# Head pairs on row halves and a ring of three banks in the second attention of a two-layer transformer kernel

## Chip, cores and metric

The kernel is one launch on one core of a Trainium2 chip. The metric is the device time of that launch in microseconds (us), lower is better. Engines are named as the profile names them: PE is TensorE's matmuls, PEld its weight loads, DVE VectorE, ACT ScalarE, POOL GpSimd, SPq the queue on which SyncE issues its DMAs. "Bank" is one of the eight PSUM banks of 128 partitions x 512 fp32.

## The reference, cut to what matters

Six stages in a row, each with a residual and a LayerNorm: attention, cross attention, a mixture of experts (layer 0), then attention, cross attention and a quantized feed-forward (layer 1). The change is in the fourth:

```python
# B, N, C = 2, 1024, 256; NUM_HEADS = 16, HEAD_DIM = 16, SCALE = 0.25
qkv = (x @ W_qkv + b_qkv).reshape(B, N, 3, NUM_HEADS, HEAD_DIM)
q, k, v = transpose(qkv, (2, 0, 3, 1, 4))
scores = einsum('bhqd,bhkd->bhqk', q, k) * SCALE
attn = softmax(scores, axis=-1)
out = einsum('bhqk,bhkd->bhqd', attn, v)
return out.transpose(0, 2, 1, 3).reshape(B, N, C) @ W_proj + b_proj
# x = layernorm(x + that)
```

## The kernel before, in words

Every stage has one function per engine (`pe_l1a`, `act_l1a`, `dve_l1a`, `pool_l1a`, `sp_l1a` for this one), and the order on each engine is the order of the code; semaphores alone tie the engines together. The stage runs 32 heads (2 batches x 16). Per head it does three things.

**Natural scores**, queries on partitions: only to find each query's largest score. `natural(x, half)` on PE writes 128 queries x 512 keys to bank 0 or 1, DVE reduces it to a column (`L1523`); after 16 of those one small reduce (`L1529`) gives the 8 columns of a head. PE transposes them ("rows", `L1305`), ACT (`L1433`) and DVE (`L1569`) split them into a high and a low part, and SPq sends both as rows into the head's query tile (`L1663`). There they meet a row of ones in the key tile, so that the next product comes with the maximum subtracted.

**Transposed scores**, keys on partitions: two matmuls of 512 queries into banks 2 and 3, or 4 and 5, and one ACT exponential over both banks (`L1440`, 128x1024) into one of three tiles `s_P`.

**Weighting**: `V1` holds 32 columns per head: 16 values, a one in column 16, zeros. Four matmuls of 256 queries, one on each 32-column group of the array, add up into bank 6 over the 8 key tiles. An fp32 matmul stands in the trace as two records, so a unit has 8. Row 16 of each group is the sum of the exponentials. ACT (`L1447`) and DVE (`L1578`) copy bank 6 into `Zs`, 32 rows per head.

A score is summed from four products (high and low part of q with high and low part of k): the query and key tiles `Qs` and `Ks` of a head carry four copies on 4 x 32 partitions, gathered by eight DMAs from the projected `TQK` (`L1645`). All matmuls of scores so use 128 rows.

A step x of the loop is a *unit*: one of 8 key or query tiles of one head, 256 in all. PE does in this order: natural half 0, transposed scores of unit x-13, natural half 1, weighting of unit x-15, then a side piece of the list `side[x]`, if there is one. Side pieces all go through bank 7, one after the other: projection of the next four heads (28 pieces in the loop, six 512-column matmuls each, evacuated by ACT `L1407` and DVE `L1503`), the values of batch 1, the rows, and for every group of four heads "sums" (the sums turned, PE then DVE reciprocal `L1546`), "spread" (ACT `L1422`), "scale" (PE turns back, DVE `L1550` multiplies), and once per batch the output projection in four groups ("project", DVE `L1554`) and the LayerNorm steps ("norm"). What is left when the loop ends runs as `rest` behind it, with the transposes `turned` of the normalized X for the next stage (four for batch 0, four for batch 1).

PE's helper `mm` is line 85, so nearly all matmuls stand under L85 and are told apart by their tiles: `PS<-s_K,s_Q` is natural, `PS<-s_Q,s_K` transposed, `PS<-s_P,s_V` the weighting.

Of the kernel before, what the change touches and what calls it, by code (L numbers as in the profile page):

```python
# [25 lines left out]
              "m_gh m_h7 m_gT c_l0 rows c_xb m_b7 m_r1 m_w1 m_r2 s_wrl s_w s_z1 s_wpl s_g0 s_g1 s_g2 s_g3 s_nr s_i s_n "  # L26
              "s_red s_za s_zv s_b7 s_rx sums s_p7 s_ip s_exp s_st s_pv s_hi s_mhd f_l0 f_l1 f_iv f_qv s_xb f_qp x_lk x_kv "
              "x_lv x_vd x_pl x_ql x_q x_fp x_ft x_ev x_z x_lo x_zT x_o x_n0 x_n1 x_t x_K0 x_K1 x_min x_s x_qh x_sub x_ex "
              "x_kT x_lh x_res f_max x_rcp x_mx x_lq x_lm f_dv f_sp f_xr f_xq f_xt f_h f_gu f_hq f_y f_yp f_cl f_e4 f_sil "
              "f_up f_hr f_hpr f_sm f_par f_s1 f_res f_hp dve").split()  # L30
# [43 lines left out]
def program(nc, A, out):  # L74
    ctx = ExitStack()
    with ctx:
# [53 lines left out]
        s_wp = sb(ctx, "s_wp", [128, 4, D])  # L130
        s_bm = sb(ctx, "s_bm", [128, 128])
# [37 lines left out]
        R_S = 4  # L169
        Qs = [sb(c, f"s_Q{i}", [128, S], FR) for i in range(R_S)]  # L170
        Ks = [sb(c, f"s_K{i}", [128, S], FR) for i in range(R_S)]
        Zs = [sb(c, f"s_Z{i}", [128, 4, S]) for i in range(2)]
        s_P = [sb(c, f"s_P{i}", [128, S]) for i in range(3)]
        nm2 = sb(c, "s_nm2", [128, 2, 8, 2])
        s_nm = sb(c, "s_nm", [128, 2, 8])
        s_mh, s_ml = sb(c, "s_mh", [8, 2, 128], FR), sb(c, "s_ml", [8, 2, 128], FR)
        s_rc = sb(c, "s_rc", [128, 2, 32])
        s_rx = [sb(c, f"s_rx{i}", [128, 512]) for i in range(2)]
# [963 lines left out]
        def pool_rest(e):  # L1142
# [25 lines left out]
            for n in sorted(plan):  # L1168
                for what in plan[n]:
                    if what[0] == "weights":  # L1170
                        split(what[1] + 3)
                    elif what[0] == "prepare":
                        e.wait_ge(s["m_y"], last_of[-1])
                        for i, (hi, lo) in enumerate(((s_vh, s_vl), (s_wh, s_wl))):
                            e.wait_ge(s["s_wrl"], 16 * (i + 1))
                            e.tensor_copy(hi[:, :], s_wr[:, :]).then_inc(s["s_w"], 1)
                            e.wait_ge(s["s_w"], 2 * i + 1)
                            e.tensor_tensor(lo[:, :], s_wr[:, :], hi[:, :].bitcast(F32), ALU.subtract).then_inc(s["s_w"], 1)
                        e.memset(V1[:, :, :, 16:32], 0.0).then_inc(s["s_z1"], 1)
                        e.wait_ge(s["s_z1"], 1)  # L1180
                        e.memset(V1[:, :, :, 16:17], 1.0).then_inc(s["s_z1"], 1)

        def sp_rest(e):
# [19 lines left out]
            for n in sorted(plan):  # L1203
                for what in plan[n]:
                    if what[0] == "weights":
                        load(what[1] + 3)
                    elif what[0] == "prepare":
                        e.wait_ge(s["m_y"], last_of[-1])
                        e.dma_start(s_wp[:, :, :], A["s_wp"].rearrange("(g p) n -> p g n", p=128)).then_inc(s["s_wpl"], 16)
                        e.dma_start(s_bm[:, :], A["s_bm"]).then_inc(s["s_wpl"], 16)  # L1210
# [8 lines left out]
        NH, LAG_M, LAG_S, LAG_P = 32, 9, 13, 15  # L1219
        N_X = 8 * NH + LAG_P  # L1220
# [4 lines left out]

        side, todo = [[] for _ in range(N_X)], []
        for x in range(N_X):
            if 0 <= x - LAG_M < 8 * NH and (x - LAG_M) % 8 == 0:
                side[x].append(("rows", (x - LAG_M) // 8))
            y = x - LAG_P  # L1230
            if 0 <= y < 8 * NH:
                if y // 8 == 15:
                    side[x].append(("values", y % 8))
                if y % 32 == 31:
                    pb, pg = y // 128, (y // 32) % 4
                    todo += [("sums", pb, pg), ("spread", pb, pg), ("scale", pb, pg, 0), ("scale", pb, pg, 1)]
                    if pg == 3:
                        for q in range(2):
                            todo += [("project", 8 * pb + j) for j in range(4 * q, 4 * q + 4)]
                            todo.append(("norm", 8 * pb + 4 * q))  # L1240
            if todo and x // 8 % 4 > 1 and x % 8 in (3, 5, 7):
                side[x].append(todo.pop(0))
            n, i = divmod(x, 8)
            if i in (2, 6) and n % 4 < 2 and n // 4 + 1 < 8:
                side[x].append(("proj", n // 4 + 1, 2 * (n % 4) + (i == 6)))
        rest = todo
        i7, i7_free, bank7 = {}, {}, {}
        for what in [w for row in side for w in row]:
            if what[0] not in ("spread", "norm"):
                i7[what], i7_free[what], bank7[what] = len(i7) + 1, len(i7), 7  # L1250
        before = {7: len(i7), 6: None}
        for i, what in enumerate(rest):
            if what[0] not in ("spread", "norm"):
                bank7[what], i7_free[what] = 7 - i % 2, before[7 - i % 2]
                i7[what] = before[7 - i % 2] = len(i7) + 1
        n_sums = {what: i for i, what in enumerate(w for w in i7 if w[0] == "sums")}

        def his(g):

            return 4 * g  # L1260

        def pe_l1a(e):
# [17 lines left out]
            def natural(x, half):  # L1280
                z, (n, i) = 2 * x + half, divmod(x, 8)
                if i == 0 and half == 0:
                    e.wait_ge(s[f"s_g{n % 4}"], 128 * (n // 4 + 1))
                if z >= 2:
                    e.wait_ge(s["s_nr"], z - 1)
                else:
                    e.wait_ge(s["s_i"], 12)
                mm(e, PS[:, half, :], Qs[n % R_S][:, i * 128:(i + 1) * 128],
                   Ks[n % R_S][:, half * 512:half * 512 + 512], True, True).then_inc(s["s_n"], 1)

            def piece(what):
# [12 lines left out]
                if what[0] == "rows":
                    t = e.transpose(PS[0:8, 7, 0:128], s_nm[:, what[1] % 2, :], ident[:, :])  # L1305
                elif what[0] == "values":
                    e.wait_ge(s[who_old], n_old)
                    t = values(1, what[1], 7)
                elif what[0] == "proj":
# [3 lines left out]
                    t = proj(g, u, 7)  # L1313
                elif what[0] == "sums":
                    _, b, g = what
                    e.wait_ge(s["s_za"], 2 * (16 * b + 4 * g + 4))
                    e.wait_ge(s["s_zv"], 2 * (16 * b + 4 * g + 4))
                    e.wait_ge(s["s_wpl"], 32)
                    for j in range(8):
                        t = mm(e, PS[:, bk, 4 * j:4 * j + 4], Zs[b][:, g, j * 128:(j + 1) * 128], s_bm[:, 16:128:32], True, True)  # L1320
                elif what[0] == "scale":
                    _, b, g, half = what
                    e.wait_ge(s["s_rx"], 2 * n_sums["sums", b, g] + half + 1)
                    for j in range(4):
                        t = mm(e, PS[:, bk, j * 128:(j + 1) * 128], s_rx[half][:, j * 128:(j + 1) * 128], ident[:, :], True, True)
                else:
                    b, j = divmod(what[1], 8)
                    e.wait_ge(s["s_b7"], i7["scale", b, 3, 1])
                    e.wait_ge(s["s_wpl"], 32)
                    for g in range(4):  # L1330
                        t = mm(e, PS[:, bk, 0:256], Zs[b][:, g, j * 128:(j + 1) * 128], s_wp[:, g, :], g == 0, g == 3)
# [5 lines left out]
            for u in range(4):  # L1337
                if u >= 2:
                    e.wait_ge(s["s_i"], u - 1)
                proj(0, u, u % 2).then_inc(s["s_ip"], 1)  # L1340
            for kt in range(8):
                e.wait_ge(s["s_i"], kt + 3)
                values(0, kt, kt % 2).then_inc(s["s_ip"], 1)
            for x in range(N_X):
                if x < 8 * NH:
                    natural(x, 0)
                extra = list(side[x])
                if extra and extra[0][0] == "rows":
                    piece(extra.pop(0))
                w = x - LAG_S  # L1350
                if 0 <= w < 8 * NH:
                    h, kt = divmod(w, 8)
                    bk = (2, 4)[w % 2]
                    if kt == 0:
                        e.wait_ge(s[f"row{h % 2}"], 256 + 32 * (h // 2 + 1))
                    if w >= 2:
                        e.wait_ge(s["s_exp"], w - 1)
                    for half in range(2):
                        t = mm(e, PS[:, bk + half, :], Ks[h % R_S][:, kt * 128:(kt + 1) * 128],
                               Qs[h % R_S][:, half * 512:half * 512 + 512], True, True)  # L1360
                    t.then_inc(s["s_st"], 1)
                if x < 8 * NH:
# [897 lines left out]
```

## Time and profile before

| | us |
|---|---|
| median of 3 runs | 2763.31 |
| lowest, highest | 2759.94, 2772.22 |
| the profiled execution, its time | 2767.74 |
| its span in the profile | 2765.9 |
| first natural matmul of the stage | at 1894.0 |
| last weighting matmul | ends at 2441.0 |
| last normalized tile of the stage | at 2479.1 |

The span is what the profile shows from the first to the last instruction; the execution's time has 1.8 us around it. Over the whole span PE is busy 91%, DVE 62%, ACT 46%, POOL 31%. A record's duration of a matmul has a latency in it: a 512-column matmul stands as 0.39 to 0.40 us but the next can start 0.22 to 0.23 us after it, so starts are to be read, not durations. The mean granted clock of TensorE over the span is 0.955 of full speed.

### The profile page before, as it was taken

To read this page: it belongs to the slowest core of one execution; us is meant where nothing else is said; L and a number is where in the kernel's file an instruction comes from. 1 tells how busy PE (TensorE), PEld (TensorE's weight loads), DVE (VectorE), ACT (ScalarE), POOL (GpSimd) and SP (SyncE) were. 2 spreads that over 40 slices of the span, in tenths; PEclk is the share of its full clock that TensorE was granted. 3 is DMA by queue.
4 is the path that set the end of the run, shared out by engine and by line. 5 is a ranking of instruction groups with operands and counts; after the bars stand their busy time and mean duration, and the time that the engine had idled before them with its cause. 6 is when DMAs were issued, how large, how long until landed. Compare 5 with 4: busy or idle time off the path is not lost.

```text
span 2765.9 us, 35667 instructions
## 1 busy us (share of the span) xinstructions
PE 2511.4 (91%) x13840; PEld 1727.1 (62%) x13840; DVE 1717.4 (62%) x3089; ACT 1282.2 (46%) x2015; POOL 867.3 (31%) x445
## 2 busy tenths in 40 slices
PE   8999998999999789899999999997999999976663
PEld 7554545744554579788888988994555555544421
DVE  5566655376665446875444344356877777847967
ACT  4555554345555144344444444442666555632342
POOL 4777774366777240102222023010200000004323
PEclk9999999999999899899999999998999999987885
DMA  2000001000000210000000010003333232210000
GB/s 74 12 22 14 12 12 43 12 12 23 12 19 1 69 61 1 31 1 31 31 31 20 12 43 9 1 1 83 74 66 70 62 66 62 47 32 9 1 0 31
DMA packets 49641, 84.23 MB, mean 30 GB/s; under 512 B 9912, under 2 KB 30016, under 8 KB 49472
## 3 DMA queue, kind: packets, MB, share of 16 engines
q1 hardware_dynamic: 49328, 81.88, 11.6%
q8 instruction: 110, 1.80, 0.3%
q14 instruction: 59, 0.48, 0.1%
q10 hardware_dynamic: 144, 0.07, 0.0%
HBM read 37.49 MB, written 2.10 MB: 14 GB/s over the span
## 4 chain that ended last, share of the span: by engine, by line
PE 75%; DVE 16%; ACT 3%; issue 3%; POOL 2%; DMA 1%; SPq 0%; ACTq 0%; DVEq 0%; POOLq 0%
PE PS L85 74%; DVE m_gl L1097 2%; DVE PS L576 2%; DVE a_QS L554 1%; ACT a_P L519 1%; DVE a_nm L568 1%; DVE s_nm L1523 1%; DVE X L271 1%; DVE x_E L1922 1%; DVE x_rd L1906 1%; DVE st_s L232 1%; DVE x_sm L1927 1%; POOL f_H L2128 1%; POOL a_sum L676 1%; ACT a_QS L473 1%
## 5 line engine op out<-in xcount | busy, mean ns | idle before, releaser
L1097 DVE TENSOR_TENSOR m_gl<-m_g,m_gh 128x512 fp32r<-128x512 f32 x288 | 258.1, 902 | 386.4 <-ACT m_g L936 386.4
L676 POOL TENSOR_TENSOR a_sum<-a_sum,a_P 128x1024 f32<-128x1024 f32 x192 | 456.6, 2378 | 128.4 <-ACT a_P L519 118.0
L519 ACT ACTIVATE a_P<-PS 128x512 f32<-128x512 f32 x512 | 290.3, 596 | 354.3 <-PE PS L85 349.5
L933 ACT ACTIVATE m_gh<-PS,cols 128x512 fp32r<-128x512 f32 x288 | 198.5, 689 | 469.6 <-PE PS L85 469.6
L1523 DVE TENSOR_REDUCE s_nm<-PS 128x1 f32<-128x512 f32 x512 | 344.8, 688 | 70.0 <-PE PS L85 67.4
L568 DVE TENSOR_REDUCE a_nm<-PS 128x1 f32<-128x1024 f32 x256 | 300.4, 1216 | 128.2 <-PE PS L85 128.2
L85 PE MATMUL PS<-m_w2h,m_gh 128*128 128x256 f32 x1152 | 324.5, 282 | 18.9 <-DVE m_gl L1097 18.7
L1440 ACT ACTIVATE s_P<-PS 128x1024 f32<-128x1024 f32 x256 | 262.1, 1024 | 165.4 <-PE PS L85 164.8
L85 PE MATMUL PS<-m_w2l,m_gh 128*128 128x256 f32 x1152 | 323.1, 280 | 0.0
L85 PE MATMUL PS<-m_w2h,m_gl 128*128 128x256 f32 x1152 | 323.0, 280 | 0.0
L85 PE MATMUL PS<-a_P,a_V 128*64 128x512 f32 x1024 | 250.9, 612 | 0.0
L85 PEld LDWEIGHTS PS<-m_w2h,m_gh 128*128 128x128 f32 x1152 | 217.7, 189 | 35.3 <-DVE m_gl L1097 23.7
L85 PE MATMUL PS<-s_K,s_Q 128*128 128x512 f32 x512 | 229.4, 450 | 8.8 <-DVE s_nm L1523 6.1
L85 PE MATMUL PS<-xh,m_w1h 128*128 128x512 f32 x576 | 231.5, 402 | 0.0
L85 PE MATMUL PS<-xh,m_w1l 128*128 128x512 f32 x576 | 227.2, 394 | 0.0
L85 PE MATMUL PS<-a_QS,a_KH 128*128 128x512 f32 x512 | 219.9, 430 | 7.8 <-ACT a_P L519 7.7
L85 PE MATMUL PS<-xl,m_w1h 128*128 128x512 f32 x576 | 226.1, 393 | 0.0
L85 PEld LDWEIGHTS PS<-m_w2h,m_gl 128*128 128x128 f32 x1152 | 218.5, 190 | 10.7
L85 PEld LDWEIGHTS PS<-m_w2l,m_gh 128*128 128x128 f32 x1152 | 218.1, 189 | 0.0
L1152 POOL CAST m_w1h<-m_raw 128x2048 fp32r<-128x2048 f32 x9 | 20.0, 2223 | 609.3 <-PE PS L85 599.9
L85 PE MATMUL PS<-a_QM,a_KL 128*128 128x512 f32 x512 | 201.8, 394 | 0.0
L936 ACT ACTIVATE m_g<-PS,cols 128x512 f32<-128x512 f32 x288 | 196.7, 683 | 0.0
(304 smaller groups left out, 4346.8 us busy)
## 6 DMA issues: line engine op xcount, KB each, us to landing
m_raw<-in_m_w SPq DMA_DIRECT2D x16, 1024.0 KB, 5.2
s_Q<-s_T SPq DMA_DIRECT2D x128, 128.0 KB, 2.4
s_K<-s_T SPq DMA_DIRECT2D x128, 128.0 KB, 2.4
a_KH<-a_KH SPq DMA_DIRECT2D x64, 128.0 KB, 2.3
a_wr<-in_w_qk SPq DMA_DIRECT2D x16, 256.0 KB, 2.9
X<-in_x SPq DMA_DIRECT2D x4, 512.0 KB, 6.6
a_P<-in_w_v SPq DMA_DIRECT2D x8, 256.0 KB, 5.8
a_P<-in_w_o SPq DMA_DIRECT2D x2, 1024.0 KB, 5.5
```

The source lines that it names most:

```text
L85: return e.matmul(o, l, r, start=start, stop=stop, skip_group_check=shared)
L232: e.bn_stats(st_s[:, j, :], X[:, j, :]).then_inc(own.sem, 1)
L271: e.tensor_scalar(X[:, j, :], X[:, j, :], st_a[:, j, 0:1], st_r[:, 0, j:j + 1], ALU.subtract, ALU.mult).then_inc(s["normed"], 1)
L519: e.activation(a_P[:, g % N_P, half * 512:half * 512 + 512], PS[:, 2 + half, :], ACT.Exp).then_inc(s["a_exp"], 1)
L568: e.tensor_reduce(a_nm[:, n % 2, 8 * a + i:8 * a + i + 1], PS[:, bk:bk + 2, :], AX.XY, ALU.max, negate=True).then_inc(s["a_max"], 1)
L576: e.reciprocal(r, r).then_inc(own.sem, 1)
L676: e.tensor_tensor(o[:, :], a_P[:, (g - 1) % N_P, :] if k == 1 else o[:, :], a_P[:, g % N_P, :], ALU.add).then_inc(s["a_add"], 1)
L933: e.activation(m_gh[r][:, :], PS[:, 4 + n % 3, :], func, bias=cols[:, bcol:bcol + 1]).then_inc(s["m_gh"], 1)
L936: e.activation(m_g0[r][:, :], PS[:, 4 + n % 3, :], func, bias=cols[:, bcol:bcol + 1]).then_inc(s["m_g0"], 1)
L1097: e.tensor_tensor(m_gl[r][:, :], m_g0[r][:, :], m_gh[r][:, :].bitcast(F32), ALU.subtract).then_inc(s["m_gl"], 1)
L1440: e.activation(s_P[w % 3][:, :].rearrange("p (a n) -> p a n", a=2), PS[:, bk:bk + 2, :], ACT.Exp, scale=0.25).then_inc(s["s_exp"], 1)
L1523: e.tensor_reduce(nm2[:, n % 2, i, half:half + 1], PS[:, half, :], AX.X, ALU.max, negate=True).then_inc(s["s_nr"], 1)
```

## The change

- **Head pairs.** A unit is now half a tile of a *pair* of heads, 256 units for 16 pairs. `Qs` and `Ks` hold one head on partitions 0 to 63 and the other on 64 to 127 (`R[0]`, `R[1]`), with 32 + 16 + 16 rows of high and low parts; the product of the two low parts is left out. Each score matmul has 64 rows. A natural unit is two matmuls, one on each row half, into a pair of banks, and one DVE reduce over 128x1024 in place of two over 128x512.
- **Ring.** The transposed scores of a unit are two matmuls (one for each head), each into the next of banks 4, 5 and 7, each with its own wait for the exponential three before it; ACT does two exponentials over 128x512, into four tiles `s_P`.
- **Weighting** in two units at a time, every second step: 2 x 4 matmuls, column group c for head c % 2 and query quarter c // 2. `V1` has ones in columns 16 to 31, so that the sum comes out sixteenfold on 16 partitions beside the 16 values. One ACT copy (128x256) per half pair into `s_zt`; then eight DMAs per pair bring values to `Zs` and sums to `Zd`, both packed 8 heads to 128 partitions.
- **Division.** DVE inverts `Zd` in pieces of 128 columns (24 in the loop, 4 of 256 behind it), POOL multiplies (`Zs` by `Zd`), for the last group DVE. "sums", "spread" and "scale" are gone, and `s_bm`; a project piece does two tiles with two groups each in place of one with four.
- **Banks.** Natural units and all side pieces except the rows take turns on the bank pairs 0-1 and 2-3; the rows go to bank 6, columns 256 to 383.
- **Lags** 16 and 18 in place of 13 and 15, so 274 steps. Only the high part of the rows is sent; `L1569` goes. The first four `turned` are side pieces now.
- **DMAs on SPq** per pair: 12 to gather (before 2 x 8), 4 for rows (before 4), 8 for `Zs` and `Zd` (before none).

The diff, cut to PE's loop, ACT's exponentials, DVE's reduce and SPq's DMAs behind each pair, in this order:

```diff
-        NH, LAG_M, LAG_S, LAG_P = 32, 9, 13, 15
-        N_X = 8 * NH + LAG_P
+        N_PR, LAG_S, LAG_P = 16, 16, 18
+        N_U = 16 * N_PR
+        N_X = N_U + LAG_P
+        RING = (4, 5, 7)
...
+            if x % 32 in (3, 7, 11, 15) and x // 32 + 1 < 8:
+                side[x].append(("proj", x // 32 + 1, (x % 32) // 4))
+            if x % 64 in range(22, 38, 2) and 86 <= x < 278:
+                side[x].append(("inverse", (x - 86) // 64, (x % 64 - 22) * 64, 128))
...
+                    who = {"natural": "s_nr", "turned": "t_xl"}.get(what[0], "s_b7")
+                    pair[what], pair_free[what], n_b7[what] = 2 * (len(used) % 2), used[-2], count[who]
...
+            for x in range(N_X):
+                w = x - LAG_S
+                if 0 <= w < N_U:
+                    p, half, kt = w // 16, (w // 8) % 2, w % 8
+                    if kt == 0:
+                        e.wait_ge(s[f"row{(w // 8) % 2}"], 256 + 32 * (w // 16 + 1))
+                    for a in range(2):
+                        if 2 * w + a >= 3:
+                            e.wait_ge(s["s_exp"], 2 * w + a - 2)
+                        mm(e, PS[:, RING[(2 * w + a) % 3], :], Ks[p % R_S][R[a], kt * 128:(kt + 1) * 128],
+                           Qs[p % R_S][R[a], half * 512:half * 512 + 512], True, True).then_inc(s["s_st"], 1)
+                if x < N_U:
+                    bk, (who, n) = pair["natural", x], pair_free["natural", x]
+                    e.wait_ge(s[who], n)
+                    for a in range(2):
+                        t = mm(e, PS[:, bk + a, :], Qs[p % R_S][R[a], i * 128:(i + 1) * 128],
+                               Ks[p % R_S][R[a], half * 512:half * 512 + 512], True, True)
+                    t.then_inc(s["s_n"], 1)
+                y = x - LAG_P
+                if y % 2 and 0 < y < N_U:
+                    for y in (y - 1, y):
+                        e.wait_ge(s["s_exp"], 2 * y + 2)
+                        for c in range(4):
+                            part = 512 * (c % 2) + 256 * (c // 2)
+                            t = mm(e, PS[32 * c:32 * c + 32, 6, 0:256], V1[:, kt, (h + c % 2) % 16, :],
+                                   s_P[y % 4][:, part:part + 256], kt == 0, kt == 7)
+                        t.then_inc(s["s_pv"], 1)
+                for what in side[x]:
+                    piece(what)
...
+                    for a in range(2):
+                        e.wait_ge(s["s_st"], 2 * w + a + 1)
+                        e.activation(s_P[w % 4][:, a * 512:a * 512 + 512], PS[:, RING[(2 * w + a) % 3], :],
+                                     ACT.Exp, scale=0.25).then_inc(s["s_exp"], 1)
...
+                    e.tensor_reduce(nm2[:, p % 2, :, i, half], PS[:, bk:bk + 2, :], AX.X, ALU.max,
+                                    negate=True).then_inc(s["s_nr"], 1)
...
+                    for c in range(4):
+                        o, sub = 32 * (p % 4) + 16 * (c % 2), c // 2
+                        for dst, r in ((Zs[g // 2], 32 * c), (Zd, 32 * c + 16)):
+                            dst = dst[o:o + 16, g % 2, :].rearrange("p (h n) -> p h n", h=2)
+                            e.dma_start(dst[:, :, sub * 256:sub * 256 + 256], s_zt[r:r + 16, q:q + 2, :]).then_inc(s[f"s_zd{p % 2}"], 16)
```

## Rows read from the trace of the kernel before

**Rows 1.** Busy time by stretch: start:end, length, five engines, granted clock, DMA share, GB/s.
```profile
1894.00:1918.00 24.00, 18.19 (x45) 9.83 (x45) 18.39 (x31) 3.62 (x5) 0.00 (x0) 0.86 0.71 168
1918.00:2426.00 508.00, 501.96 (x3423) 274.57 (x3423) 402.32 (x737) 303.96 (x375) 24.75 (x24) 1.00 0.28 62
...
2441.00:2479.20 38.20, 26.37 (x140) 22.32 (x136) 20.09 (x70) 5.26 (x10) 0.00 (x0) 0.89 0.00 1
2479.20:2560.00 80.80, 53.64 (x218) 39.05 (x219) 58.58 (x86) 22.10 (x38) 33.66 (x20) 0.73 0.13 35
```

**Rows 2.** Timeline of PE over one plain unit: start us, duration us, instructions.
```profile
2072.14 0.64 PE L85 MATMUL PS<-s_P,s_V 128*32 128x256 f32 x8
2072.71 0.50 PE L85 MATMUL PS<-s_K,s_Q 128*128 128x512 f32 x1
2073.05 0.63 PE L85 MATMUL PS<-s_Q,s_K 128*128 128x512 f32 x2
2073.51 0.40 PE L85 MATMUL PS<-s_K,s_Q 128*128 128x512 f32 x1
2073.83 0.42 PE L85 MATMUL PS<-s_P,s_V 128*32 128x256 f32 x4
```

**Rows 3.** Groups of the loop, 1894 to 2441.2: count, busy us, mean ns, idle before.
```profile
L1523 DVE TENSOR_REDUCE s_nm<-PS 128x1 f32<-128x512 f32 x512 | 344.8, 688 | 70.0 <-PE PS L85 67.4
L1440 ACT ACTIVATE s_P<-PS 128x1024 f32<-128x1024 f32 x256 | 262.1, 1024 | 165.4 <-PE PS L85 164.8
...
L85 PEld LDWEIGHTS PS<-s_K,s_Q 128*128 128x128 f32 x512 | 96.7, 189 | 111.5 <-DVE s_nm L1523 78.3 <-issue 20.2 <-DMA s_K<-s_T 1.7
...
L1503 DVE SCALAR_TENSOR_TENSOR s_T<-PS,cols,s_T 128x512 fp32r<-128x512 f32 x28 | 20.8, 742 | 0.0
L1407 ACT ACTIVATE s_T<-PS,cols 128x512 fp32r<-128x512 f32 x28 | 19.3, 691 | 51.1 <-PE PS L85 51.1
L85 PE MATMUL PS<-s_wp,s_Z 128*128 128x256 f32 x64 | 16.0, 392 | 0.0
L85 PE MATMUL PS<-ident,s_rx 128*128 128x128 f32 x96 | 13.9, 288 | 0.0
L85 PE MATMUL PS<-s_bm,s_Z 128*128 128x4 f32 x112 | 13.6, 254 | 0.0
...
L1529 DVE TENSOR_REDUCE s_nm<-s_nm 128x8 f32<-128x16 f32 x32 | 5.4, 170 | 1.1
```

**Rows 4.** Timeline of the loop's end, where no natural scores are left.
```profile
2437.32 0.73 PE L85 MATMUL PS<-s_Q,s_K 128*128 128x512 f32 x2
2437.98 0.64 PE L85 MATMUL PS<-s_P,s_V 128*32 128x256 f32 x8
2438.09 1.03 ACT L1440 ACTIVATE s_P<-PS 128x1024 f32<-128x1024 f32 x1 [0.21 <-PE PS L85]
2438.55 0.73 PE L85 MATMUL PS<-s_Q,s_K 128*128 128x512 f32 x2
2439.22 1.82 PE L85 MATMUL PS<-s_P,s_V 128*32 128x256 f32 x24
```

**Rows 5.** Groups of the whole span, by shape, that other stages show.
```profile
L568 DVE TENSOR_REDUCE a_nm<-PS 128x1 f32<-128x1024 f32 x256 | 300.4, 1216 | 128.2 <-PE PS L85 128.2
L576 DVE RECIPROCAL PS<-PS 128x256 f32<-128x256 f32 x64 | 108.1, 1733 | 48.7 <-PE PS L85 48.3
L519 ACT ACTIVATE a_P<-PS 128x512 f32<-128x512 f32 x512 | 290.3, 596 | 354.3 <-PE PS L85 349.5
```

**Rows 6.** DMAs that read the projected tiles: ns min/median/max of an issue, landing time.
```profile
L1645 SPq DMA_DIRECT2D s_Q<-s_T x128: 521/590/2152, 1887.1 to 2387.7; - x128
...
DMA to landing us min/median/max: 2.3/2.4/4.1
```

**Rows 7.** Timeline behind the loop, its two ends: the last copies and the last normalization.
```profile
2441.11 0.89 DVE L1578 COPY s_Z<-PS 32x256 f32<-32x256 f32 x2 [8.49 <-PE PS L85]
...
2468.72 0.75 DVE L1554 TENSOR_TENSOR X<-PS,X 128x256 f32<-128x256 f32 x2
...
2477.73 1.38 DVE L271 TENSOR_SCALAR X<-X,st_a,st_r 128x256 f32<-128x256 f32 x4
```

More of the change, by code:

```diff
@@ L1227, in program @@
         for x in range(N_X):
-            if 0 <= x - LAG_M < 8 * NH and (x - LAG_M) % 8 == 0:
-                side[x].append(("rows", (x - LAG_M) // 8))
+            if x >= 9 and (x - 9) % 8 == 0 and (x - 9) // 8 < 2 * N_PR:
+                side[x].append(("rows", (x - 9) // 8))
             y = x - LAG_P
[L1231 to L1240, printed above, removed]
@@ L1241, in program @@
-            if todo and x // 8 % 4 > 1 and x % 8 in (3, 5, 7):
-                side[x].append(todo.pop(0))
[L1243 to L1260, printed above, removed]
+            if y % 2 == 1 and 120 <= y < 128:
+                side[x].append(("values", y - 121))
@@ new lines, in program @@
+            if x in (229, 237, 245, 253):
+                side[x].append(("turned", (x - 229) // 8))
+        rest = []
+        for i in range(4):
+            rest += [("inverse", 3, 256 * i, 256), ("divide", 256 * i), ("project", 8 + 2 * i)]
+        rest = [rest[i] for i in (0, 1, 3, 4, 2, 6, 7, 5)] + [("norm", 8)] + [rest[i] for i in (9, 10, 8, 11)] + [("norm", 12)]
+        i7, pair, pair_free, n_b7, used = {}, {}, {}, {}, [("s_i", 12), ("s_i", 12)]
+        count = {"s_b7": 0, "s_nr": 0, "t_xl": 16}
@@ new lines, in dve_l1a @@
+            for x in range(N_X):
+                if x == 40:
+                    slow.append(round_steps(e, own, range(6)))
+                if x < N_U:
+                    p, i, half = x // 16, (x // 2) % 8, x % 2
+                    e.wait_ge(s["s_n"], x + 1)
+                    if x % 16 == 0 and p >= 2:
+                        e.wait_ge(s["s_red"], 2 * p - 2)
+                    bk = pair["natural", x]
+                    e.tensor_reduce(nm2[:, p % 2, :, i, half], PS[:, bk:bk + 2, :], AX.X, ALU.max,
+                                    negate=True).then_inc(s["s_nr"], 1)
+                    if x % 8 == 7:
+                        q = x // 8
+                        e.wait_ge(s["s_nr"], x + 1)
+                        if q >= 2:
+                            e.wait_ge(s["s_p7"], i7["rows", q - 2])
+                        e.tensor_reduce(s_nm[:, q % 2, :].rearrange("p (a i) -> p a i", a=2),
+                                        nm2[:, p % 2, :, 4 * (q % 2):4 * (q % 2) + 4, :], AX.X, ALU.min).then_inc(s["s_red"], 1)
+                if late:
+                    what = late.pop()
+                    if what[0] == "turned":
+                        turned(what[1], pair[what])
+                    else:
+                        low(what[1], what[2], pair[what]).then_inc(s["s_b7"], 1)
+                for what in side[x]:
+                    piece(what)
+                pump(slow, 2)
@@ L1589, in dve_l1a @@
             pump(slow, 99)
-            for i in range(4):
-                turned(i, i % 2)
             for what in rest:
```

442 lines of the change are left out of this document (183 added, 259 removed).

## The prediction

> **What bounds the kernel now.** First the busy time by stretch [rows 1]. From 1918 to 2426 us PE is busy 502 of 508 us at full granted clock, DVE 402, ACT 304. This stage is 547 us from its first natural matmul to its last weighting, and PE is its wall. Then the groups [rows 3]: ACT's exponentials waited 165 us for PE, DVE's reduces 67 us for PE, PE next to nothing for others. Then one plain unit, by starts and not by durations [rows 2]: weighting at 2072.14, the two transposed and two natural matmuls in between, weighting again at 2073.83, so 1.69 us a unit. A 512-column matmul behind a like one takes 0.22 to 0.23 (2073.05 to 2073.51 is two), the change from 128x128 to 128x32 tiles 0.33 (2073.51 to 2073.83), so 0.11 of it is the switch. Where natural scores are gone a unit takes 1.23 [rows 4].
>
> These make up the loop: lead-in 24.0 [rows 1], 243 units at 1.69 = 410.7, last 15 at 1.23 = 18.5; 547.1 less these leaves 93.9 for all side pieces. That agrees with what PE does there: 28 projections of 6 matmuls at 0.23 = 38.6, sums, scale and project 13.6 + 13.9 + 16.0 = 43.5 [rows 3], the rest rows and values.
>
> **The change part by part.**
>
> *What PE has to do in two units.* Weighting: 24 records in a row take 1.82, and the last one's latency is some 0.16 of it, so 8 take 0.55 and 16 take 1.10 [rows 4]. Score pairs on row halves: no row shows two matmuls on different rows at once. Bounds: 0.22 a pair (fully side by side, as the four column groups of the weighting are: eight 256-column fp32 records in 0.57 [rows 2, 4]) and 0.43 (one after the other). I take 0.22, because the nearest row, the column groups, does overlap. The Trainium skill, "TensorEngine Tiling (Array Packing)", Key Properties, says that different tiles load weights and run matmuls in parallel, and that changing the mode drains the array. By it a pair is 0.22; the drain agrees with the 0.11 of rows 2, overlap of rows no trace here shows.
>
> *What ACT and DVE have to do.* A unit has two exponentials of 512 at 596 ns = 1.19 us [rows 5] in place of one of 1024 ns [rows 3]; DVE one reduce of 1216 ns [rows 5] in place of 2 x 688 = 1.38 [rows 3]. So ACT needs 2.38, DVE 2.43 for two units, PE 4 x 0.22 + 1.10 + 2 switches = 2.2 to 3.1. None is the wall by far; PE's fixed order then is.
>
> *The chain through the ring.* Put the end of exponential (w-1, head 0) at 0, w odd in the order of weighting. It frees the bank for (w, head 1). PE: start 0.1 (semaphore, an estimate: from PE's end at 2438.05 to ACT's start it was 0.04 [rows 4], and a weight load comes first), 0.32 the natural pair, 0.54 switch, 0.66 weighting of two units 1.10, switch 0.10, next unit's transposed scores at 1.86. Their exponential can start 0.43 later (a record's 0.39 plus the semaphore), at 2.29, and ends at 2.89. ACT had only 1.79 us of scores in the three banks, so it idles 0.5. The exponential ending at 2.89 frees the bank for (w+2, head 1), which is where we began. **Period 2.89 for two units, 1.445 a unit.** DVE needs 2.43 in it and fits. Without the natural pair it is 2.67, 1.33 a unit.
>
> *Side pieces.* 93.9 less sums and scale 27.5, less half of the project pieces 8.0 [rows 3]. Plus one more switch (0.11) for each of 28 projections and 32 rows, 6.6; plus four transposes moved in, 2.4; plus 24 inversions on DVE of half of 1733 ns = 20.8 [rows 5], of which DVE's slack hides half (0.46 us per two units): 10.4; plus LayerNorm and rounding steps on a DVE with less slack, 8 (estimate); plus ACT's row and bank-6 copies beyond its idle 0.5, 5. Sum 91. A projection now takes a turn on the natural banks: low part 742 ns [rows 3] on DVE and a natural unit one turn later; inside the 1.4 us that PE is away DVE has one reduce pending, so I charge nothing more. It costs up to 1 us each, 28 us, if the buffers run dry; that is in the range.
>
> *Loop.* Lead-in: 16 units without exponentials at DVE's pace, 16 x 1.27 (1.216 and a gap of 0.05) = 20.3, plus 6 for its projections (before: 24.0 less 13 x 1.38). Middle 240 x 1.445 = 346.8. Sides 91. End 18 x 1.33 = 23.9. Together 488, against 547.1: **-59**.
>
> *Start.* The first natural unit now waits for 12 gathers, not 8; SPq issues one every 0.63 (0.59 and a gap) [rows 6]: **+2.5**.
>
> *Behind the loop.* Before, 38 us from the last weighting to the last normalized tile [rows 7], DVE busy 20 [rows 1]. Now: ACT copy 0.6, eight DMAs 5.1, landing 2.4 [rows 6], then DVE with four inversions of 1733 (6.9), four products (1.5), and what it did, less the four `turned` and the scaling, some 15: 31.6. **-6**, between -10 and +3 (PE cold in the DMA wait).
>
> *DMAs and POOL.* SPq issues 24 per pair = 15.1 us, of 23.1 for 16 units. The rows of the second half queue behind 12 gathers (7.6), take 1.3 to issue and 2.4 to land: 11.3 after step 15 of the pair, wanted nine units later, at 13.0. Hidden, with 1.7 to spare; at 1.25 us a unit it would not be. POOL's products are off the chain: it was busy 25 of 508 us [rows 1], and a project piece that needs one comes many units later. Dropping `L1569` and the 32-partition copies relieves DVE, which isn't the wall: nothing. `L1529` stays, 32 x 170 ns.
>
> **Sum:** -59 + 2.5 - 6 = -62.5 against the profiled execution, 2767.7 (span 2765.9 and 1.8 around it), so 2705; that execution stood 4.4 above the median 2763.3, so **2701 us**.
>
> **The rivals.**
>
> *B, pairs don't overlap.* A pair takes 0.43, whether the array or the weight loads serialize it: each load stands as 189 ns [rows 3] and a pair has two. The chain grows by 0.22 per two units to 3.11, 1.555 a unit: +26, 2727. For it: no row shows the overlap, and the loads stay 128 columns wide. Against: the column groups.
> The Trainium skill, "TensorE: Matmul & The Clock Gate", LDWEIGHTS, says that a load's time goes by columns and not by rows, 107 ns for 128; halving the rows then saves no load time. By that figure two loads fit under one 0.22 matmul and the period stays 1.445. The trace has loads of 189 as recorded, but with their latency, so it doesn't decide.
>
> *C, the chain is slacker than I draw it* and DVE's own work is the wall: 256 x 1.216 = 311, low parts 21, small reduces 5, inversions 21, others about 25: 383, plus the last 18 units 24 = 407. -140 and the ends: 2620. For it: the ring holds 1.79 us of exponentials, and two natural units can be pending. Against: in-order PE must finish 1.1 us of weighting between two banks.
>
> *D, slower: the clock falls.* For the first time in this loop PE would wait often. The mean granted clock was 1.00 where PE is busy 99%, 0.86 at 76%, 0.89 at 69%, 0.73 at 66% [rows 1]; the two levels are 2.4 and 1.2 GHz. PE's part of the chain, 1.86 of 2.89, doubles at 1.2: +0.93 a unit. With half of the loop at 1.2: +112, sides +36, so 2849. The change is lost once the period passes 1.705 (62.5 / 240 more), that is with 28% of the loop at 1.2. Against: in the lead-in's 76% busy most is recorded latency, two starts of 0.22 in 1.38 us; here starts fill 2.2 of 2.89.
>
> *E, SPq is late.* The eight new DMAs cut 16 partitions into 1 KB pieces, which no row shows. At the 0.59 median they fit. At the longest issue seen, 2.15 [rows 6], a pair needs 17.2 + 10.1 = 27.3 us against 23.1: +67 over 16 pairs, 2768, no change. It decides from about 1.6 us an issue.
>
> **How the numbers follow.** Forecast 0.50, B 0.20, C 0.13, D 0.06, E 0.08; 0.03 for anything else on the faster side. A measurement of this kernel can tell about 0.5% (14 us). Faster: 0.50 + 0.20 + 0.13 + 0.03 = 0.86; same 0.08 (E); slower 0.06 (D). The range 2640 to 2745 takes in the bounds of the forecast (sides -10 to +28, pair 0.22 to 0.43, tail -4 to +9), all of B and the near half of C; it leaves out D, E and the rest of C, 0.2.
>
> **What would show it.** Right: plain pairs of units repeat every 2.9 us; ACT's exponentials at 596 idle about 0.5 us every second unit, released by PE; the two matmuls of a natural pair start within 0.05 us; PE near 80% busy at clock 1.00; last weighting some 490 us after the first natural matmul. B: starts within a pair 0.22 apart, period 3.1 or more. C: reduces back to back at 1.22. D: granted clock under 0.9. E: PE's waits released by the DMA of `s_mh` or by the gathers, 2 us and more per half pair. A period above 3.4 us for two units with none of these would break the account of the chain itself.

## The result and the profile after

12 runs each, side by side: 2766.57 us before, 2776.44 after (2771.68 to 2785.24), ratio 1.0039 with a 95% interval of 1.0024 to 1.0054. The change is **slower by 0.4%**; the forecast was 2701 with a range of 2640 to 2745. The profiled execution of the changed kernel has a span of 2779.9, 14.0 more than before.

Busy time by stretch, changed kernel (columns as in rows 1): lead-in up to the first transposed matmuls, loop, its end, and what lies behind it up to the next stage.

```profile
1900.90:1936.00 35.10, 23.94 (x62) 12.16 (x62) 21.59 (x22) 3.98 (x6) 1.49 (x2) 0.60 0.23 55
1936.00:2436.00 500.00, 428.25 (x3117) 205.56 (x3121) 347.94 (x401) 279.21 (x568) 30.75 (x29) 0.89 0.21 41
2436.00:2459.40 23.40, 19.29 (x195) 8.12 (x193) 1.40 (x2) 17.39 (x35) 0.00 (x0) 1.00 0.05 12
2459.40:2490.50 31.10, 13.25 (x44) 9.82 (x40) 18.18 (x47) 0.98 (x3) 0.00 (x0) 0.71 0.04 9
```

Against [rows 1] PE, DVE and ACT have less to do (PE 428 us of 500 where it had 502 of 508), only POOL has more (31 us where it had 25). Yet the loop did not get shorter, and the granted clock, 1.00 before, is 0.89 on average, in the lead-in 0.60 for 0.86. Where the 14.0 us are:

| stretch | before | after | difference | forecast |
|---|---|---|---|---|
| last matmul of the stage before starts | 1867.8 | 1872.7 | +5.0 | 0 |
| from there to the first natural matmul | 26.2 | 28.2 | +2.0 | +2.5 |
| first natural to end of last weighting | 547.1 | 558.5 | +11.4 | -59 |
| to the last normalized tile | 38.1 | 34.8 | -3.3 | -6 |
| rest of the kernel | 286.8 | 285.7 | -1.1 | 0 |

The first line is scatter of the unchanged stages between executions: in the profile of one of the kernels below that same matmul starts at 1860.4. Start and tail came as forecast, within 3 us. The loop is 70 us off.

The exponentials and reduces on the page of the changed kernel:

```profile
L1525 DVE TENSOR_REDUCE s_nm<-PS 128x2 f32<-128x1024 f32 x256 | 310.2, 1219 | 142.8 <-PE PS L85 142.2
L1408 ACT ACTIVATE s_P<-PS 128x512 f32<-128x512 f32 x512 | 264.4, 602 | 102.9 <-PE PS L85 102.7
```

1219 and 602 ns, against 1216 and 596 taken from [rows 5]: the prices were right. DVE now waits 142 us for PE (67 before, rows 3): the engine that makes the others wait is still PE, though it is itself idle. So who makes PE wait? First two plain units, timeline of the changed kernel (one line of ACT, the rest PE):

```profile
2108.57 1.07 PE L85 MATMUL PS<-s_P,s_V 128*32 128x256 f32 x16
2109.57 0.50 PE L85 MATMUL PS<-s_Q,s_K 64*128 64x512 f32 x2
2109.91 0.40 PE L85 MATMUL PS<-s_K,s_Q 64*128 64x512 f32 x2
2110.14 0.39 PE L85 MATMUL PS<-s_Q,s_K 64*128 64x512 f32 x1
2110.16 2.07 ACT L1408 ACTIVATE s_P<-PS 128x512 f32<-128x512 f32 x4 [1.99 <-PE PS L85]
...
2110.81 0.49 PE L85 MATMUL PS<-s_Q,s_K 64*128 64x512 f32 x1 [0.28 <-ACT s_P L1408]
2110.82 0.71 PE L85 MATMUL PS<-s_K,s_Q 64*128 64x512 f32 x2
2111.46 1.07 PE L85 MATMUL PS<-s_P,s_V 128*32 128x256 f32 x16
```

From 2108.57 to 2111.46 is 2.89 us, the forecast's 2.89. Two matmuls on the two row halves stand as one line of 0.50 or 0.40, and the next kind starts 0.23 to 0.34 later: they overlap in full. The wait of 0.28 is for the exponential that frees the next bank of the ring. This is the chain, and it is the whole of a plain pair of units. Now a pair with a projection and the one behind it:

```profile
2029.81 1.07 PE L85 MATMUL PS<-s_P,s_V 128*32 128x256 f32 x16
2030.81 0.50 PE L85 MATMUL PS<-xh,s_wh 128*128 128x512 f32 x1
...
2032.39 0.51 PE L85 MATMUL PS<-s_Q,s_K 64*128 64x512 f32 x2
2032.50 0.69 ACT L1390 ACTIVATE s_T<-PS,cols 128x512 fp32r<-128x512 f32 x1 [1.94 <-PE PS L85]
...
2033.17 1.23 DVE L1525 TENSOR_REDUCE s_nm<-PS 128x2 f32<-128x1024 f32 x1 [2.03 <-PE PS L85]
2033.73 0.49 PE L85 MATMUL PS<-s_Q,s_K 64*128 64x512 f32 x1 [0.37 <-ACT s_P L1408]
2034.31 0.74 DVE L1467 SCALAR_TENSOR_TENSOR s_T<-PS,cols,s_T 128x512 fp32r<-128x512 f32 x1
2035.11 0.50 PE L85 MATMUL PS<-s_K,s_Q 64*128 64x512 f32 x2 [0.89 <-DVE s_T L1467]
2035.54 1.93 PE L85 MATMUL PS<-s_P,s_V 128*32 128x256 f32 x16
...
2037.40 0.79 PE L85 MATMUL PS<-s_Q,s_K 64*128 64x512 f32 x2
...
2039.62 1.07 PE L85 MATMUL PS<-s_P,s_V 128*32 128x256 f32 x16
```

This takes 5.73 us (2.83 above plain), and the pair behind it 4.08. Read it from the wait of 0.89 backwards: the natural matmuls need the bank pair in which the projection lies; DVE reads it last (`L1467`, 2034.31 to 2035.05); but DVE's order has the next natural reduce first (2033.17), which PE could only feed after the projection. Everything in the pair waits in a ring. Then the weighting at 2035.54 lasts 1.93 and not 1.07. Busy time of the same stretches:

```profile
2029.81:2035.54 5.73, 4.47 (x32) 2.31 (x31) 3.21 (x4) 3.39 (x7) 0.00 (x0) 1.00 0.61 129
2035.54:2039.62 4.08, 4.08 (x27) 1.77 (x25) 2.18 (x2) 1.33 (x3) 0.00 (x0) 0.58 0.23 53
2039.62:2045.35 5.73, 4.47 (x31) 2.31 (x30) 3.45 (x5) 3.37 (x7) 0.00 (x0) 1.00 0.03 6
2045.35:2049.56 4.21, 4.21 (x27) 1.87 (x25) 2.42 (x2) 2.10 (x6) 0.00 (x0) 0.59 0.00 1
```

The granted clock, the number behind the five engines, is 1.00 with the projection and 0.58 to 0.59 behind it: most of that pair ran at the lower of the two levels, 1.2 GHz. Of the 24 pairs behind a projection in the loop 17 have a clock of 0.57 to 0.72; the other 7 have 1.00. Five of these stand behind a pair of the same 5.73 to 5.74 us, the plain pair at 2108.57 above among them. So the clock does not fall behind every such stop, and nothing here says behind which. By the starts of the weightings, the 24 pairs of units in the loop that carry a projection take 6.33 us on average, the 24 behind them 3.94; by the forecast's terms a projection alone makes it 4.4 (2.89, 1.38 for six matmuls, 0.11 for a switch) and 2.9. In the kernel below that has neither this wait nor the next one the same pairs take 4.77 and 3.15, other side pieces included, so 24 x 2.3 = 56 us are waits and slow clock.

A last stall, once in each of three groups of heads; waits in the loop of the changed kernel:

```profile
DVE s_Zd L1499 <- DMA s_Zd<-s_zt: 13.4, 3, 4.9
```

and the first of the three in the timeline:

```profile
2081.89 0.95 DVE L1499 RECIPROCAL s_Zd<-s_Zd 128x128 f32<-128x128 f32 x1 [4.82 <-DMA s_Zd<-s_zt]
...
2083.98 0.80 PE L85 MATMUL PS<-s_K,s_Q 64*128 64x512 f32 x2 [4.28 <-DVE s_nm L1525]
```

The first inversion of a group comes in DVE's order before its sums have landed, and PE stands 4.3 us behind DVE.

So there are three theories: **1**, the shared natural banks and DVE's order behind them; **2**, the clock that falls behind most of these stops; **3**, the late DMA. The rival to all is that the side pieces and the inversions simply cost more work.

### The profile page after: what moved, and what is told of

Same layout as the page of the kernel before. It is cut to its first block, busy times and chain, and to the rows that moved or that the text cites. A ratio compares the mean times of both kernels' runs of the same rounds, so it can differ in the third digit from the quotient of the medians.

```text
span 2779.9 us, 34891 instructions
## 1 busy us (share of the span) xinstructions
PE 2436.5 (88%) x13518; PEld 1651.5 (59%) x13520; DVE 1672.6 (60%) x2737; ACT 1259.5 (45%) x2223; POOL 873.8 (31%) x450
## 4 chain that ended last, share of the span: by engine, by line
PE 70%; DVE 18%; ACT 4%; issue 3%; SPq 2%; POOL 1%; DMA 1%; ACTq 0%; DVEq 0%; POOLq 0%
PE PS L85 68%; DVE m_gl L1096 2%; DVE s_nm L1525 2%; DVE PS L575 2%; ACT s_P L1408 2%; DVE a_QS L553 1%; ACT a_P L518 1%; DVE a_nm L567 1%; SPq L1605 1%; DVE X L270 1%; DVE x_E L1894 1%; DVE x_rd L1878 1%; DVE s_T L1467 1%; SPq L1637 1%; DVE x_sm L1899 1%
## 5 line engine op out<-in xcount | busy, mean ns | idle before, releaser
L1525 DVE TENSOR_REDUCE s_nm<-PS 128x2 f32<-128x1024 f32 x256 | 310.2, 1219 | 142.8 <-PE PS L85 142.2
L567 DVE TENSOR_REDUCE a_nm<-PS 128x1 f32<-128x1024 f32 x256 | 300.4, 1216 | 127.1 <-PE PS L85 127.1
L1408 ACT ACTIVATE s_P<-PS 128x512 f32<-128x512 f32 x512 | 264.4, 602 | 102.9 <-PE PS L85 102.7
L85 PE MATMUL PS<-s_Q,s_K 64*128 64x512 f32 x512 | 188.6, 512 | 35.6 <-ACT s_P L1408 35.3
L85 PE MATMUL PS<-s_K,s_Q 64*128 64x512 f32 x512 | 148.8, 481 | 55.3 <-DVE s_T L1467 27.2
```

The source lines that it names most:

```text
L85: return e.matmul(o, l, r, start=start, stop=stop, skip_group_check=shared)
L567: e.tensor_reduce(a_nm[:, n % 2, 8 * a + i:8 * a + i + 1], PS[:, bk:bk + 2, :], AX.XY, ALU.max, negate=True).then_inc(s["a_max"], 1)
L1408: e.activation(s_P[w % 4][:, a * 512:a * 512 + 512], PS[:, RING[(2 * w + a) % 3], :], ACT.Exp, scale=0.25).then_inc(s["s_exp"], 1)
L1525: e.tensor_reduce(nm2[:, p % 2, :, i, half], PS[:, bk:bk + 2, :], AX.X, ALU.max, negate=True).then_inc(s["s_nr"], 1)
```

## The experiments

Each edit is against the changed kernel if nothing else is said. "Plain" and "projection" are the pairs of units from weighting to weighting, read as above.

### The low part first

```diff
                 elif what[0] == "proj":
-                    late.append(what)
+                    low(what[1], what[2], pair[what]).then_inc(s["s_b7"], 1)
```

> Edit: DVE takes the low part of a projection (the read that frees the natural bank pair) before the next natural reduce, not behind it. Theory 1 (shared natural banks): a step pair with a projection takes 5.73 us in the changed kernel's trace where a plain one takes 2.90; 1.5 of the 2.83 is PE's own work and the rest the wait for that low part. It ends about 1.1 us earlier here: step pair about 4.6, PE's wait for the low part from 0.89 to under 0.2, stage 28 x 1.1 = 31 us shorter, 2745. If the clock also stays up behind it (theory 2), the following step pair falls from 4.1 to about 3.0 as well, 2715. Rival (the shared banks don't matter, PE's extra work does): 5.73 stays, 2776.

2725.44, ratio 0.9861 (0.9827 to 0.9895): 50 us less by moving 28 instructions of DVE one place forward.

```profile
2021.35 1.07 PE L85 MATMUL PS<-s_P,s_V 128*32 128x256 f32 x16
...
2024.76 0.75 DVE L1467 SCALAR_TENSOR_TENSOR s_T<-PS,cols,s_T 128x512 fp32r<-128x512 f32 x1 [1.88 <-ACT s_T L1390]
2025.27 0.50 PE L85 MATMUL PS<-s_Q,s_K 64*128 64x512 f32 x1 [0.37 <-ACT s_P L1408]
...
2025.57 0.49 PE L85 MATMUL PS<-s_K,s_Q 64*128 64x512 f32 x2
2025.99 1.07 PE L85 MATMUL PS<-s_P,s_V 128*32 128x256 f32 x16
...
2029.10 1.07 PE L85 MATMUL PS<-s_P,s_V 128*32 128x256 f32 x16
```

The projection's pair takes 4.64 (expected 4.6), PE no longer waits for the low part, and the pair behind it 3.11, weighting back to 1.07. Theory 1 stands. The clock fell behind none of the 24 projections here, so the 50 us hold what theory 2 has to price as well. The time lies between the two expected numbers: three pairs with late sums are left, and they grew from 7.7, 6.5 and 8.6 us to 9.2, 7.6 and 9.7.

### Filling the wait

```diff
-                        mm(e, PS[:, RING[(2 * w + a) % 3], :], Ks[p % R_S][R[a], kt * 128:(kt + 1) * 128],
-                           Qs[p % R_S][R[a], half * 512:half * 512 + 512], True, True).then_inc(s["s_st"], 1)
+                        for _ in range(4 if a and any(z[0] == "proj" for z in side[x - 2]) else 1):
+                            t = mm(e, PS[:, RING[(2 * w + a) % 3], :], Ks[p % R_S][R[a], kt * 128:(kt + 1) * 128],
+                                   Qs[p % R_S][R[a], half * 512:half * 512 + 512], True, True)
+                        t.then_inc(s["s_st"], 1)
```

> Edit: in the step in which PE waits for the low part of a projection, it runs the transposed matmul of the second head four times into the same bank, so three of them (0.66 us) fill the wait of 0.89 without changing a result. Theory 2 (the granted clock falls behind each projection because PE stands still, 1.00 then 0.58 to 0.60 in the trace, and costs 1.2 us a time): the step pair behind a projection goes from 4.1 to about 2.9, the fourth projection of a group from 7.6 to 5.7, in all some 25 to 35 us less, about 2745, with more matmuls. Rival (the slow pair behind a projection has another cause, such as the banks): no change, or up to 28 x 0.3 = 8 us more.

2747.12, ratio 0.9942 (0.9921 to 0.9963): 29 us *less* by doing *more* matmuls (27 by the two ratios).

```profile
2024.90 1.19 PE L85 MATMUL PS<-s_Q,s_K 64*128 64x512 f32 x4 [0.38 <-ACT s_P L1410]
2026.29 0.50 PE L85 MATMUL PS<-s_K,s_Q 64*128 64x512 f32 x2 [0.19 <-DVE s_T L1469]
2026.72 1.07 PE L85 MATMUL PS<-s_P,s_V 128*32 128x256 f32 x16
...
2029.61 1.07 PE L85 MATMUL PS<-s_P,s_V 128*32 128x256 f32 x16
```

The projection's pair stays at 5.75, since the wait for the low part still ends when it did; the pair behind it takes 2.89 in place of 4.08, and the 7.6 of a group's fourth projection is 5.7. In the loop the clock fell behind 17 of 24 projections before and behind none now, and the banks are as they were, so the slow pairs behind projections are the clock's alone. Theory 2 stands, and its price there is these 27 to 29 us; they are a part of the 50 of the first edit, not added to them.

### Inversions six steps later

```diff
-            if x % 64 in range(22, 38, 2) and 86 <= x < 278:
-                side[x].append(("inverse", (x - 86) // 64, (x % 64 - 22) * 64, 128))
+            if x % 64 in range(28, 44, 2) and 92 <= x < 278:
+                side[x].append(("inverse", (x - 92) // 64, (x % 64 - 28) * 64, 128))
```

> Edit: the 8 inversions of a group start 6 steps later. Theory: in the changed kernel DVE waits 4.8 us in its own order for the DMA of the sums at the first inversion of each of three groups, and PE behind it 4.3 (step pair 7.7 for 2.9), clock 0.52 for 9 us after that. Here that wait is gone: 3 x 4.5 = 13 us, and 3 to 8 more of the clock, 2757 to 2763. Rival (the inversions themselves, 0.94 us of DVE each, are what costs): the stall moves along, under 4 us gained.

2757.32, ratio 0.9969 (0.9952 to 0.9987), 0.7% or 19 us under the changed kernel. The wait on the DMA is gone from the list of waits of the loop, and in two of the three groups plain pairs with an inversion in them take 2.90 us. There the inversions cost nothing; their place did. In the third group, where DVE has LayerNorm steps as well, pairs with an inversion still take 2.9 to 6.5. Theory 3 stands.

### Both natural matmuls on one row half

The maxima of each pair's second head are left out; the first head's are used for it.

```diff
-                        t = mm(e, PS[:, bk + a, :], Qs[p % R_S][R[a], i * 128:(i + 1) * 128],
-                               Ks[p % R_S][R[a], half * 512:half * 512 + 512], True, True)
+                        t = mm(e, PS[:, bk + a, :], Qs[p % R_S][R[0], i * 128:(i + 1) * 128],
+                               Ks[p % R_S][R[0], half * 512:half * 512 + 512], True, True)
```

> Edit: both matmuls of a natural pair read the first row half, so the maxima of the second head are left out and the first head's used in their place; all else as the changed kernel. Theory (row halves overlap; a pair costs PE one 512-column matmul): starts within the pair go from together to 0.22 apart, a plain step pair from 2.90 to about 3.11, the stage 120 x 0.21 = 25 us longer, 2800. Rival (PE has slack enough in a step pair to take it): 2.90 stays, 2776.

2819.93, ratio 1.0201 (1.0165 to 1.0237): 44 more than the changed kernel, but not as expected. Timeline of a plain pair and busy time of its loop:

```profile
2161.97 0.51 PE L85 MATMUL PS<-s_Q,s_K 64*128 64x512 f32 x2
2162.31 0.62 PE L85 MATMUL PS<-s_K,s_Q 64*128 64x512 f32 x2
2162.77 0.94 PE L85 MATMUL PS<-s_Q,s_K 64*128 64x512 f32 x2
```

```profile
1935.00:2480.00 545.00, 491.55 (x3107) 247.93 (x3104) 342.23 (x399) 278.91 (x562) 30.41 (x28) 0.82 0.19 37
```

The two now follow each other (0.62 for 0.40, and the next kind starts 0.46 later where it was 0.23), but a plain pair still takes 2.90 to 2.91. The step of the expectation that fell is that the chain has no room for it. In the second unit the natural pair never was together: its second matmul shares rows with the transposed one of the second head and went behind it already (0.71 at 2110.82 above). In the first unit the added 0.23 came out of PE's wait for the ring: the wait of 0.28 is gone, and the two transposed matmuls of the second unit stand as one line without a gap (2162.77). So this kernel shows the overlap by its absence, but prices neither the expected 25 us nor rival B, in which no pair overlaps. What grew are the pairs with projections (6.2 to 8.5 for 5.7 to 7.7, where no values are computed in them) and the share of the slow clock, 0.82 for 0.89.

### A ring of two, and a bank of their own for the projections

```diff
-        RING = (4, 5, 7)
+        RING = (4, 5)
...
+                elif what[0] == "proj":
+                    count["s_b7"] += 1
+                    pair[what], pair_free[what], n_b7[what] = 7, own7, count["s_b7"]
+                    own7, i7[what] = ("s_b7", count["s_b7"]), len(i7) + 1
...
-                        if 2 * w + a >= 3:
-                            e.wait_ge(s["s_exp"], 2 * w + a - 2)
+                        if 2 * w + a >= 2:
+                            e.wait_ge(s["s_exp"], 2 * w + a - 1)
```

> Edit: the ring of the transposed scores has two banks (4, 5), and bank 7 belongs to the projections, as before the change; the rest is the changed kernel. Theory (the shared natural banks cost the projections their 2.8 us; the ring sets the plain step pair by the chain of the prediction): with two banks the chain is 0.1, 0.22 + 0.22 + 0.12, 1.10 of weighting, 0.10, 0.43 to the next exponential, two exponentials of 0.60, 3.49 us for a plain step pair in place of 2.90, and a step pair with a projection only its own 1.6 longer, near 5.1, with the pair behind it plain. Plain pairs +0.59 x 120 = +71, projections -28 x 1.2 and the clock behind them -28 x 1.0: 2785 in all. Rival (the ring's size doesn't matter): plain stays 2.90, 2715.

2780.19, ratio 1.0055 (1.0037 to 1.0073). Two plain units:

```profile
2003.94 1.07 PE L85 MATMUL PS<-s_P,s_V 128*32 128x256 f32 x16
...
2006.18 0.98 PE L85 MATMUL PS<-s_Q,s_K 64*128 64x512 f32 x2 [0.51 <-ACT s_P L1412]
...
2007.33 1.07 PE L85 MATMUL PS<-s_P,s_V 128*32 128x256 f32 x16
```

Plain 3.39 (expected 3.49), with a projection 5.07 (5.1), behind it 3.40 to 3.60. The third bank is worth 0.49 us on every plain pair, 59 us in 120; a bank of their own for the projections, with the clock that stays up behind them (0.96 in the loop), gives back all but 4 of these. The change traded the one for the other. The same bank shortens the lead-in, 33.3 us in the changed kernel, to about the forecast's 26:

```profile
1888.00:1915.20 27.20, 19.69 (x59) 10.04 (x59) 20.79 (x21) 2.33 (x4) 0.00 (x0) 0.69 0.31 70
```

### One unit of weighting in every step

```diff
-                if y % 2 and 0 < y < N_U:
-                    for y in (y - 1, y):
+                if 0 <= y < N_U:
+                    for y in (y,):
```

> Edit: weighting of one unit in every step, not of two in every second; all else the changed kernel. Theory (the plain step pair is the chain through the ring, in which 1.1 us of weighting stands between two banks): with 0.55 in its place ACT never runs dry, a plain pair becomes PE's own work, 2 x (0.10 + 0.22 + 0.22 + 0.12 + 0.55), 2.45 us instead of 2.90: 120 x 0.45 = 54 us less, 2720, the projections' waits staying. Rival (each switch of tile shape costs more than 0.11, or DVE's 1.22 a unit with its gaps is the wall): 2.7 to 2.9 a pair, 2750 to 2776.

2711.90, ratio 0.9807 (0.9786 to 0.9828), 64 less than the changed kernel (54 expected). PE's work from one start of weighting to the next:

```profile
2002.35 0.64 PE L85 MATMUL PS<-s_P,s_V 128*32 128x256 f32 x8
...
2002.92 0.50 PE L85 MATMUL PS<-s_Q,s_K 64*128 64x512 f32 x2
...
2003.25 0.40 PE L85 MATMUL PS<-s_K,s_Q 64*128 64x512 f32 x2
...
2003.58 0.64 PE L85 MATMUL PS<-s_P,s_V 128*32 128x256 f32 x8
```

1.23 a unit, 2.46 a pair, against 2.45 expected, although the tile shape now changes twice as often, and PE no longer waits in it. DVE's two reduces of 1.22 would allow hardly less. The weighting of two units at once is what let the ring run dry.

### Low part first and late inversions

> Edit: the low part of a projection first on DVE, and the inversions 6 steps later, together. If the two losses are separate stalls they add: 2725 less 13 to 20, so 2708 (in the kernel with the first edit alone three step pairs of 7.6 to 9.7 us were left). Rival (with the first edit the DMA wait is hidden by nothing less and moves to another place): 2725.

2696.61, ratio 0.9756 (0.9739 to 0.9773): 28.8 below the first edit alone, more than the 13 to 20 expected: in the kernel with the first edit alone the three pairs with late sums took 9.2, 7.6 and 9.7 us and the one behind each 4.9, which is 24 above plain. Its natural and its weighting matmuls:

```profile
L85 PE MATMUL PS<-s_K,s_Q x512: 383/394/793, 1894.8 to 2351.5; 64*128 64x512 f32 x171
```

```profile
L85 PE MATMUL PS<-s_P,s_V x2048: 379/379/634, 1931.7 to 2375.0; 128*32 128x256 f32 x187
```

The loop is 480.6 us (1894.8 to 2375.0 and a record's 0.4), where the forecast has 488, and the granted clock in it 0.61 in the lead-in and 0.99 behind. Its pairs with a projection take 4.65, where no values are computed in them; the forecast's terms give 4.4.

### All three

> Edit: all three, one unit of weighting in every step, low part first, inversions late. If chain, bank wait and DMA wait are separate, 2708 less 54 = 2655. Rival (DVE becomes the wall: 256 x 1.22 and 70 us of pieces, 382 us of a loop that is then 440): each piece on DVE shows in full, 2680.

**2662.45, ratio 0.9633 (0.9614 to 0.9651)**, the best but one of the kernels made here, 3.7% under the kernel before. It is 7 us above the 2655 of the expectation. Two entries of its waits, 1930 to 2330:

```profile
DVE s_nm L1525 <- PE PS L85: 16.5, 30, 1.8
...
PEld PS L85 <- DMA s_Q<-s_mh: 9.2, 5, 3.1
```

DVE's reduces wait 17 us where they waited 142: now PE and DVE are close to even (357 and 325 us busy in 375). And PE waits for the DMA of the row of maxima, five times: the forecast has it hidden with 1.7 us to spare at 1.445 a unit and not at 1.25, and at 1.23 it shows.

### The lead-in filled

Against the kernel with all three:

```diff
-                    for a in range(2):
+                    for a in (0, 1) * (4 if x < 16 else 1):
                         t = mm(e, PS[:, bk + a, :], Qs[p % R_S][R[a], i * 128:(i + 1) * 128],
```

> Edit: the kernel with single weighting, low part first and late inversions; in the 16 units of the lead-in, where PE has only natural pairs, each pair is run four times into the same banks, so results stay. Theory (the lead-in takes 31 us because PE stands still behind DVE and the granted clock falls to 0.61, which makes its four projections 1.4 us longer each): clock near 1.00 there, lead-in from 30.9 to about 25 us, 2657 against 2662. Rival (DVE's 16 reduces, the low parts and the waits between them make the 31 us): the repeated matmuls delay each reduce by 0.66 and the lead-in grows to 33 or more, 2665.

2658.53, ratio 0.9625 (0.9606 to 0.9644), which overlaps the interval of the kernel without it. Its lead-in:

```profile
1893.60:1922.50 28.90, 26.82 (x153) 16.70 (x153) 21.61 (x21) 2.33 (x4) 0.00 (x0) 0.92 0.28 65
```

The clock rose from 0.61 to 0.92, but the lead-in fell only from 30.9 to 28.9, not to 25. Both theories hold in part: the first projection takes 1.60 us for 2.86, but the repeated matmuls make the reduces later. Not tried: an order of the lead-in that has fewer waits.

## Why the prediction was wrong

**Right, to a few per cent.** The plain pair: 2.89 forecast, 2.89 to 2.91 measured; without natural scores 2.67 and 2.66 to 2.68. The overlap of row halves (rival B) and both new durations. Start +2.5 and +2.0, tail -6 and -3.3. Here the trace agrees with the Trainium skill, "TensorEngine Tiling (Array Packing)", Key Properties, that different tiles work in parallel. It agrees also with the Trainium skill, "TensorE: Matmul & The Clock Gate", LDWEIGHTS, that a weight load goes by columns: 64 rows x 128 columns take 183 and 186 ns here (medians), where 128 rows took 188 and 187 in the kernel before.

That the plain pair agrees to 0.01 us is partly luck. Read from the lines at 2108.57 to 2111.46, the chain's terms are: end of an exponential to PE's start 0.05 (forecast 0.10); from there to the weighting 0.65 (0.56); weighting and switch 1.00 (1.20); start of the scores to start of their exponential 0.59 (0.43); the exponential 0.60 (0.60). The path is the one forecast; the errors of its terms, up to 0.20, cancel.

**The step that failed** is *Side pieces*: "A projection now takes a turn on the natural banks ... inside the 1.4 us that PE is away DVE has one reduce pending, so I charge nothing more. It costs up to 1 us each, 28 us, if the buffers run dry." It costs 1.3 us each in the same pair of units (5.73 for 4.4), and behind 17 of 24 about another 1.2 (4.1 for 2.9). Even the bound that was named, 28 us, is too small, since it has no slow clock in it. I had counted DVE's pending work and not followed who frees the bank: PE's projection, then ACT's copy, then DVE's *next reduce*, then the low part. The wait was to be read from the diff: `late.append`, and the pop behind the next reduce, were there already before the change, but before it only bank 7 hung on them, a bank that no score needs. The first edit puts a price on it, 50 us with the clock behind it, of which filling the wait gave back 27 to 29. With the late DMA it makes the 80 us between the changed kernel and the one without either stop (2776.44 and 2696.61).

**Rival D** had the clock's mechanism and missed its place and size. I argued it away with "starts fill 2.2 of 2.89", which is right for the plain pair (clock 1.00 from 2006 to 2030) and says nothing of a pair in which PE stands 0.37 and then 0.89. It was a price on most stops of a side piece, 27 to 29 us in all by the filling, not on the loop as a whole.

**Rival E** looked at SPq's issues. These were 0.59 as in [rows 6], and a pair's 24 fit. The eight new DMAs did hurt, elsewhere: the first inversion of a group stands in DVE's order 5 steps behind their issue. The forecast gave 24 inversions a price and none of them a due time. 19 us.

**The lead-in** took 33.3 us for the forecast's 26, at clock 0.60. It has the same step in it: with the low part first it takes 30.9, and with a bank of their own for the projections 27.2.

With the first and the third of these stops out of the kernel, which leaves the change itself whole, the time is 2696.61 for the forecast's 2701. This nearness too has luck in it: its lead-in is 4.6 us longer than forecast, and its side pieces take 78 us (449.6 behind the lead-in less 240 x 1.45 less 23.9) for the forecast's 91. Which of the terms in that 91 are too large was not taken apart. The account of what the change does was right; the account of who waits in it was short.

## What to carry to other kernels

Where two kinds of work come to share a buffer, follow the freeing of it through every engine's program order to the last reader, and move that reader ahead of work which itself depends on the engine that waits; here that was one line and 1.8%. A step that gets its data by DMA needs a due time in its engine's order as well as a price. On TensorE a stop costs its own length and can cost the slow clock behind it (here behind 17 of 24), so a wait is to be priced with both.

## What the hardware showed unexpectedly

- **Matmuls that change nothing made the kernel 27 to 29 us faster.** PE stood 0.37 and 0.89 us in a projection's pair, and the next 4.1 us ran at a granted clock of 0.58, weighting 1.93 for 1.07; so it went behind 17 of 24 projections. With three repeated matmuls in the second wait (0.38 and 0.19 left) the clock stayed at 1.00 behind all 24. The 0.28 of each plain pair never brought it down. Length alone does not decide: stops of 0.29 and 0.91 us (at 2420.53 and 2421.93) left the clock at 1.00.
- **Matmuls on the two row halves overlap across kinds too**: the transposed matmul of the second head and the natural one of the first start 0.01 us apart (2110.81 and 2110.82).
- **A change of tile shape cost no more when there were twice as many**: with one unit of weighting at a time a unit takes 0.57 (weighting), 0.33 (transposed) and 0.33 (natural), 1.23 us without a wait of PE. Each 0.33 is 0.23 and a switch of 0.10, as in the changed kernel.
